# An AdaLN block with a recurrence and a gated cell, one core: gate f's place, and the order of three engines in the last units

## The reference

```
sa, ca, ga, sb, cb, gb = (silu(cond) @ wmod) in six parts; ga, gb kept at least 0.25 away from zero
h  = layernorm(x) * (1 + ca) + sa
# sublayer 1: h_t = tanh(h_{t-1} @ A.T + x_t @ B.T) over 1024 steps; y_t = h_t @ C.T
z  = y + h;  x1 = x + ga * (layernorm(z) * gamma + beta)
h  = layernorm(x1) * (1 + cb) + sb
# sublayer 2, a scan over the 8 batch rows, each with all 1024 positions as its batch:
f = sigmoid(h wf.T + c uf.T + bf); i = sigmoid(h wi.T + c ui.T + bi); g = tanh(h wc.T + c uc.T + bc)
c = f * c + i * g
out = x1 + gb * tanh(h wo.T + c_final uo.T + bo)
```

## Time and profile before

| | |
|---|---|
| median of the runs | 563.35 us |
| profiled execution | 562.41 us, span 560.5 us |
| TensorE clock granted | 0.996 of full speed over the span |
| PE busy | 542.3 us (97%) |
| DVE, ACT, POOL busy | 391.0, 342.1, 342.5 us (70, 61, 61%) |
| chain that ended last | PE 84%, issue 4%, POOL 4%, DMA 2%, ACT 2%, DVE 1% |

### The profile page before, as it was taken

How to read it: one execution, slowest core, us unless ns; L and a number is a source line. 1 busy time by engine, 2 the same in 40 slices (tenths; PEclk the granted TensorE clock), 3 DMA queues, 4 the chain that set the end, 5 groups by cost and what they waited for, 6 DMA issues and landing times.

```text
span 560.5 us, 13419 instructions
## 1 busy us (share of the span) xinstructions
PE 542.3 (97%) x4616; PEld 531.1 (95%) x4616; DVE 391.0 (70%) x908; ACT 342.1 (61%) x862; POOL 342.5 (61%) x475
## 2 busy tenths in 40 slices
PE   6999999999989999999999999999999999999994
PEld 3899999999989999999999999999999999999983
DVE  5999878886757665555876676776677666665763
ACT  3777777775456555465765556666666566667551
POOL 4767777660366444454776666677666766678354
PEclk9999999999999999999999999999999999999998
DMA  8656444435243222222133333433332343233254
GB/s 275 179 190 200 139 150 151 136 94 158 88 133 105 67 71 74 74 76 77 56 103 103 104 102 94 124 113 112 95 95 95 95 123 115 86 99 91 63 116 152
DMA packets 58514, 64.10 MB, mean 114 GB/s; under 512 B 5408, under 2 KB 49736, under 8 KB 58448
## 3 DMA queue, kind: packets, MB, share of 16 engines
q1 hardware_dynamic: 58448, 63.26, 37.0%
HBM read 46.44 MB, written 16.81 MB: 113 GB/s over the span
## 4 chain that ended last, share of the span: by engine, by line
PE 84%; issue 4%; POOL 4%; DMA 2%; ACT 2%; DVE 1%; SPq 1%; POOLq 0%; DVEq 0%; ACTq 0%
PE psI L1559 13%; PE psOF L1559 13%; PE psG L1559 13%; PE psWR L1617 7%; PE psWR L1518 7%; PE psWR L1429 4%; PE psWR L1464 4%; PE psOF L1464 4%; PE psOF L1429 4%; PE psOF L1545 3%; PE psC L1545 3%; PE psT L1596 2%; PE psC L1481 1%; PE psT L1481 1%; PE psOF L1504 1%
## 5 line engine op out<-in xcount | busy, mean ns | idle before, releaser
L649 POOL TENSOR_TENSOR hin<-hin,uvec 128x256 f32<-128x256 f32 x64 | 50.8, 815 | 30.8 <-ACT hin L811 30.1
L1260 DVE SCALAR_TENSOR_TENSOR lo<-psT,cb1T,hi 128x256 fp32r<-128x256 f32 x60 | 26.3, 479 | 50.2 <-ACT hi L876 50.2
L656 POOL TENSOR_TENSOR hsl<-hs,hsh 128x512 fp32r<-128x512 f32 x24 | 31.0, 1291 | 49.5 <-DVE state L1276 32.7
L690 POOL TENSOR_TENSOR zn<-zn,tA 128x512 f32<-128x512 f32 x32 | 45.6, 1426 | 12.1 <-ACT zn L849 12.1
L849 ACT ACTIVATE zn<-state,nmA,rstdA 128x256 f32<-128x256 f32 x64 | 35.0, 594 | 27.5 <-POOL nmA L680 27.5
L1518 PE MATMUL psWR<-hs,AT 128*128 128x128 f32 x368 | 49.6, 275 | 0.9 <-ACT hs L838 0.9
L1140 DVE TENSOR_TENSOR pre<-psWR,state 128x256 f32<-128x256 f32 x44 | 18.5, 420 | 45.8 <-PE psWR L1518 45.6
L838 ACT ACTIVATE hs<-pre 128x256 f32<-128x256 f32 x44 | 18.4, 418 | 50.6 <-DVE pre L1140 50.4
L663 POOL TENSOR_TENSOR xin<-xin,tA 128x512 f32<-128x512 f32 x32 | 41.4, 1292 | 12.7 <-DMA tA<-rows_d 12.7
L1094 DVE SCALAR_TENSOR_TENSOR hin<-xin,mvA,uvec 128x256 f32<-128x256 f32 x56 | 41.6, 782 | 9.4 <-DMA h_park<-hin 8.9
L1518 PEld LDWEIGHTS psWR<-hs,AT 128*128 128x128 f32 x368 | 45.2, 191 | 1.2 <-ACT hs L838 1.1
(11 more groups left out here) (381 smaller groups left out, 2304.9 us busy)
## 6 DMA issues: line engine op xcount, KB each, us to landing
h_park<-hin SPq DMA_DIRECT2D x32, 256.0 KB, 2.2
hin<-h_park SPq DMA_DIRECT2D x64, 128.0 KB
xin<-in_L_attn_x_dram SPq DMA_DIRECT2D x64, 128.0 KB
tA<-rows_d SPq DMA_DIRECT2D x32, 256.0 KB, 4.4
out_dram<-state SPq DMA_DIRECT2D x64, 128.0 KB
xin<-in_L_attn_x_dram SPq DMA_DIRECT2D x28, 256.0 KB, 2.8
tW<-rows_d SPq DMA_DIRECT2D x32, 128.0 KB, 3.1
tG<-rows_d SPq DMA_DIRECT2D x24, 128.0 KB, 3.6
```

What stands on the lines that cost most here:

```text
L649: pool.tensor_tensor(h, h, sa, ALU.add).then_inc(a_h, 1)
L690: pool.tensor_tensor(two(zn[:, :]), two(zn[:, :]), both(tA[:, m % 2, 0:D]), ALU.mult).then_inc(s_zg, 1)
```

## The change

Four edits. Gate f is written by ACT to `gf` in SBUF instead of back into psF; DVE's product reads and writes `gf`, and PE waits for ACT's gate f (s_f) in place of DVE's product (s_fc). In units without steps (u from 32 on) DVE does `row_stats` ahead of the output's sum; POOL does the second norm's factors ahead of the add of U, which becomes a function `add_u`. In units 33 to 35 PE's C projection stands behind the x parts of gates f and g. The U product of the unit without steps (n = 24) stands ahead of Wo's product.

```diff
@@ POOL, unit2
-                if has(o + 1, 0, LAST):
-                    if o >= 0:
-                        pool.wait_ge(s_fin, o + 1)
-                    pool.wait_ge(s_wx, o + 2)
-                    pool.wait_ge(s_u, (o + 1) // NB + 1)
-                    t = wx[:, (o + 1) % NWX, :]
-                    pool.tensor_tensor(t, t, uvec[:, :], ALU.add).then_inc(s_ua, 1)
+                if u < PAIRS:
+                    add_u(o + 1)
                 if norm:
                     pool.wait_ge(s_mvB, 2 * m + 2)
...
                     pool.tensor_tensor(nmB[:, :], ngB[:, :], rstdB[:, :], ALU.mult).then_inc(s_nB, 1)
+                if u >= PAIRS:
+                    add_u(o + 1)
                 if has(m, 1, NU - 2):
                     xg_of(m + 1)
+
+            def add_u(o):
+                if not has(o, 0, LAST):
+                    return
+                if o > 0:
+                    pool.wait_ge(s_fin, o)
+                pool.wait_ge(s_wx, o + 1)
+                pool.wait_ge(s_u, o // NB + 1)
+                t = wx[:, o % NWX, :]
+                pool.tensor_tensor(t, t, uvec[:, :], ALU.add).then_inc(s_ua, 1)
@@ ACT, gate
-                dst, src, fn, done = ((psF[:, :], psF, ACT.Sigmoid, s_f), (psI[:, :], psI, ACT.Sigmoid, s_i),
+                dst, src, fn, done = ((gf[:, :, :].rearrange("p m n -> p (m n)"), psF, ACT.Sigmoid, s_f), (psI[:, :], psI, ACT.Sigmoid, s_i),
@@ DVE, kept_part
-                dve.tensor_tensor(gf[:, :, :], psF[:, :].rearrange("p (m n) -> p m n", m=H), prev, ALU.mult).then_inc(s_fc, 1)
+                dve.tensor_tensor(gf[:, :, :], gf[:, :, :], prev, ALU.mult).then_inc(s_fc, 1)
@@ DVE, unit2
                     scaled_rows(m)
+                if has(m, 1, NU - 1) and not rec:
+                    row_stats(m)
                 if has(o, 0, LAST):
...
-                if has(m, 1, NU - 1):
+                if has(m, 1, NU - 1) and rec:
                     row_stats(m)
@@ PE, gate_x
-                    pe.wait_ge((s_fc, s_c, s_g)[i], (n, n, 2 * n)[i])
+                    pe.wait_ge((s_f, s_c, s_g)[i], (2 * n, n, 2 * n)[i])
@@ PE, unit2
-                elif here:
+                elif here and u <= PAIRS:
                     project(here[0])
                 if x:
                     gate_x(n, 0)
                     gate_x(n, 2)
+                if here and u > PAIRS:
+                    project(here[0])
...
+                turn = has(n, NB, NU - NB) and n % NB == 0
+                if turn and not rec:
+                    times_uo(n // NB - 1)
                 if x and not rec and n < HELD:
                     times_wo(n)
...
-                if has(n, NB, NU - NB) and n % NB == 0:
+                if turn and rec:
                     times_uo(n // NB - 1)
```

## The result

The changed kernel takes **572.05 us** (571.1 to 572.85) against 563.15 beside it, a ratio of 1.0154, 95% interval 1.0142 to 1.0167. The prediction was 565.2 with 562.8 to 566.8: right in sign, wrong by 7 us, outside its range. The profiled execution (571.1 us, the shortest of the six) has a span of 569.2 us for 560.5, and this difference of 8.7 is what has to be found.

The account below looks back on a forecast made before the run. PE was taken as the bound, held at 525.33 by c(29) behind a POOL, ACT and DVE loop. 0.2 + 1.15 + 0.45 = +1.8 us on the median 563.35 gave 565.2 us, range 562.8 to 566.8.

Parts of the forecast that it names:

- What bounds the kernel: PE's time is the kernel's; late units have a longer POOL, ACT, DVE loop, and c(29) holds PE at 525.33.
- Part 1: Gate f in SBUF: PE's waits for gf go, 1.37 us at most, but count nothing before 525.33; step units cost 0.
- Part 2: PE's C projections and U product moved: a 0.95 us gain against 1.15 from a new wait at gate f, n = 25.
- the 0.2 of the sum: Net cost of moving PE's C projections and U product: +0.2 us.
- Part 3: Second norm ahead on DVE and POOL: the loop comes later by +1.15 us, then +0.45 us, and so does c(29).
- +1.15 for the moved add: POOL: L663 starts behind the add of U, so unit 38's nmA is 1.15 us later.
- +0.45: Next turn of the loop, set by mvB: L663 0.55 us later, less 0.10 idle time, so +0.45 us.
- a shift of the loop that doesn't grow stays hidden: Units 32 to 37: PE's unit with Wo, 10.4 us at most, is longer than the loop and hides its shift.
- nmB of unit 37 was to be still behind ngB: Profile sign on POOL: nmB still waits for ACT's ngB, with the add of U right after it.
- Rival 3: Step units: gf held beside POOL delays DVE's recurrence sum and PE; +7 us, 570; 10 in 100.
- Rivals 1 and 2: First: all named waits go, 561.2 us, 12 in 100. Second: shift partly absorbed, +0.6 to +1.1, 564.2, 18 in 100.

Follow-up runs that it names:

- the Wo sum first: Changed kernel, with DVE's Wo sum (one SBUF input) issued ahead of the output's sum in units without steps: 570.9 us, ratio 1.0126.
- e1_gate: Kernel before with only gate f in SBUF, DVE's product reading it there and PE waiting for ACT's gate f: 563.83 us, ratio 1.0009.
- short sum: Changed kernel with DVE's Wo sum ahead of the output's sum, which adds only 2 of 512 columns in units without steps: 567.28 us, ratio 1.0066.
- both remedies: Changed kernel with POOL's x sum ahead of the second norm's factors (units without steps) and DVE's end-state check ahead of lo (unit 39): 565.06 us, 1.0030.
- check moved: Changed kernel with DVE's four instructions of the end-state check put ahead of lo in unit 39: 567.41 us, ratio 1.0078.

## Why the prediction was wrong

- **What bounds the kernel: half right.** The loop through POOL, ACT and DVE was the right one. But c(29) held PE at 525.33 by 0.2 us at the most: the part starts 0.56 us behind the first transpose, for 0.35 where nothing holds it, and with c 0.98 earlier it starts 0.02 earlier. In the changed kernel the exit that the loop takes to PE first is xn, not c. Before, xn ended 1.5 us ahead of its transposes in unit 37 (495.24 and 496.73), but only 0.26, 1.01 and 0.61 in the three units without Wo (505.22 and 505.48; 514.53 and 515.54; 524.16 and 524.77). That slack was not in the working.
- **Part 1: right in what it said.** gg rows of gate f have a mean of 472 ns (475 predicted), gf has a median of 690 and a maximum of 1162 ns (up to 1524 in the four units that start a group), no PE row waits for DVE's gf, and units with steps cost nothing. It counted the hold of gf by wide POOL instructions, but not that gf itself holds the short ones: rstdB, 0.32 a turn. The trace of before already had such a row: veA at 441.52 took 0.55 us for 0.20, behind a clo that began at 441.36.
- **Part 2: right for PE, wrong for the loop.** PE is 0.20 us late at gate i's x part of n = 25 (476.95 for 476.75), the 0.2 of the sum. With a wait of 0.82 for the 1.08 predicted, and PE already 0.06 late at 454.8, that the total agrees is partly luck. But the U product ahead of the transposes put x1 1.91 us back (0.35 of it was there a unit earlier), and the change without the moves is 1.8 us faster. The "+0.2" looked at what PE waits for and not at who waits for PE.
- **Part 3: the step that failed.** Its +1.15 for the moved add is confirmed: nmA of unit 34 is 1.19 later (465.78 for 464.59). What failed is "+0.45" for the next turn, which measured 10.81 - 9.23 = 1.58, and with it "a shift of the loop that doesn't grow stays hidden" in units 32 to 37: at 10.85 the turn is over PE's unit of 10.0 to 10.35 with Wo as well, so the shift grew from unit 34 on, and PE stood for 1.9 to 2.1 in each unit without Wo. The missing terms are the statistics' own wait (0.24) and the holds of veB, rstdB and veA (1.11 in all). One of the prediction's signs says the same: nmB of unit 37 was to be still behind ngB, and it starts at 506.94, with ngB done at 505.37.
- **Not in the sum at all:** the U product's delay of x1, the held compare (1.10) and the half clock (1.28). The last two came with the shift. Adding the price of each move in a straight line can't find these: a shift changes who stands beside whom.
- **Rivals.** Rival 3 gave 570, the nearest time, for a reason that is refuted: PE never waits in the units with steps. Rivals 1 and 2 needed slack that POOL didn't have.

The lock itself was in the prediction, named from the Trainium skill (SBUF — State Buffer, "Who interferes with whom"), but I priced it for wide POOL instructions only. The rows above show it for 128x2 ones, and the two experiments that change what DVE does beside them show that it is the wide DVE instruction that does it. The same section says that tensor_scalar can enter modes that take the shared ports too; the trace agrees, 0.29 us alone and 1.39 to 1.42 beside POOL, with a single SBUF input.

## What to carry to other kernels

When a change brings a short instruction of POOL forward to start right behind a DVE result, look at what DVE does next: with two wide SBUF inputs there, the short one lasts until the wide one is through. Price a moved instruction on both sides, who it waits for and who is queued behind it on every loop through its engine, and compare the new turn of the loop with the bound engine's unit in every stage, not only in the one where it shows today. A shift of a few us makes new neighbours; reserve for that in the range.

## What the runs showed of the hardware

- A POOL instruction of 128x2 elements issued behind a DVE instruction with two wide SBUF inputs ends just after it: 0.55 to 0.71 us for 0.20, and 0.06 us behind the DVE instruction's end in veB at 494.37, veA at 498.75 and, with the Wo sum first, nmB at 496.76. rstdB, 0.70 by itself, took 1.02 when it started 0.22 us behind gf. Issued clearly first it is not held, nor does it hold DVE (before: rstdA at 485.62 took 0.70 and clo at 485.81 0.69). 0.02 us ahead was not enough: in `e1_gate` nmA at 476.30 took 0.76, beside a clo that began at 476.32.
- Taking one holder away moves the hold to the next short instruction (veB and rstdB, then nmB) if DVE starts another such instruction just ahead of it.
- A DVE instruction with one SBUF input and its output in SBUF is held beside wide POOL work as well: 1.39 to 1.42 for 0.29.
- PE's clock fell to 0.50, 1.2 of 2.4 GHz, after some stands and not after others of like length. It fell after 2.11 and 1.89 us with four transposes between them (changed kernel), after 1.69 and 1.62 likewise (short sum, at 0.50 from 528.87 past 534 us), after one of 2.10 (both remedies), after one of 1.88 (check moved, 0.50 from 510 to 512), after one of 1.99 (without POOL's swap, 0.50 from 523 to 526), and after one of 3.39 (moves alone, 475 to 477 us at 0.50). It did not after 1.89 and 1.95 (changed kernel), nor after 1.79 (check moved), nor after one of 2.48 (gate f back in psF, 521.5 to 523.5 us at 1.00). The length of the last stand alone does not tell, and what does stays open. In the changed kernel the fall cost 1.3 us over twelve matmuls; with the check moved the one at 510 us was hidden, since PE was to wait for the loop anyway.
